# Other orders for the five engines' steps, planned with longer VectorE and GpSimd durations for the first batch

## What is computed

```python
scale, shift = jnp.split(emb @ W_emb + b_emb, 2, axis=-1)
xn = _rms_norm(x, g_norm) * (1.0 + scale) + shift
q, k, v = ...                     # of xn @ W_qkv, 16 heads of 64
q, k = _rms_norm(q, g_q), _rms_norm(k, g_k)
attn = softmax(einsum('bhqd,bhkd->bhqk', q, k) * d ** (-0.5))
o = einsum('bhqk,bhkd->bhqd', attn, v)   # back to (b, n, dim)
return x + o + o @ W_out
```

## Time and profile before

| | us |
|---|---|
| Median of 3 runs | 2257.38 |
| Lowest and highest | 2257.04, 2260.83 |
| Profiled execution, its time: the span from the first to the last instruction, the only one given for it | 2255.9 |
| TensorE busy in the span | 2176.2 |
| VectorE | 1748.6 |
| ScalarE | 1411.7 |
| GpSimd | 931.4 |

### The profile page before, as it was taken

One profiled execution on the slowest core, in us unless ns is written; L12 is line 12 of the kernel. 1 busy time (PEld: TensorE's weight loads), 2 busy tenths in 40 slices (PEclk: granted clock), 3 DMA queues, 4 the chain that ended last, 5 costly groups with the idle time before them and its releaser, 6 DMA issues.

```text
span 2255.9 us, 39472 instructions
## 1 busy us (share of the span) xinstructions
PE 2176.2 (96%) x13392; PEld 1992.2 (88%) x13392; DVE 1748.6 (78%) x3511; ACT 1411.7 (63%) x3077; POOL 931.4 (41%) x1241
## 2 busy tenths in 40 slices
PE   7788789999999999999999999999999999999999
PEld 3676678999999999999999999999999999999989
DVE  4799988678985699767986689857897569876786
ACT  4577766467854577546864578646775458754663
POOL 3866674235532345223541246312553325422330
PEclk9899999999999999999999999999999999999999
DMA  7655464777556765568555675566654775656842
GB/s 299 238 212 226 188 224 147 269 269 254 192 187 241 271 218 196 175 236 289 207 202 197 230 285 192 189 238 242 230 205 165 254 281 199 203 192 227 294 157 103
DMA packets 141528, 497.55 MB, mean 221 GB/s; under 512 B 14864, under 2 KB 61968, under 8 KB 140304
## 3 DMA queue, kind: packets, MB, share of 16 engines
q1 hardware_dynamic: 141328, 495.03, 61.7%
HBM read 425.77 MB, written 69.21 MB: 219 GB/s over the span
## 4 chain that ended last, share of the span: by engine, by line
PE 77%; DVE 11%; issue 4%; DMA 4%; ACT 3%; POOL 1%; SPq 0%; DVEq 0%; ACTq 0%
PE proj_bank L597 16%; PE proj_bank L599 16%; PE proj_bank L598 16%; PE flip_bank L721 8%; PE pv_bank L732 5%; PE pv_bank L733 5%; PE score_bank L713 4%; PE score_bank L714 4%; DMA w_ring<-qkv_store 2%; DVE neg_max L1069 2%; DVE probs L1075 2%; PE score_bank L686 2%; DVE pt_lo L1079 1%; ACT pt_hi L866 1%; ACT probs L860 1%
## 5 line engine op out<-in xcount | busy, mean ns | idle before, releaser
L597 PE MATMUL proj_bank<-w_ring,xa_hi 128*128 128x384 f32 x1792 | 626.5, 350 | 21.0 <-DVE xa_lo L1058 7.6
L599 PE MATMUL proj_bank<-w_ring,xa_lo 128*128 128x384 f32 x1792 | 606.4, 338 | 0.0
L598 PE MATMUL proj_bank<-w_ring,xa_hi 128*128 128x384 f32 x1792 | 605.7, 338 | 0.0
L860 ACT ACTIVATE probs<-score_bank,neg_max 128x512 f32<-128x512 f32 x512 | 352.1, 690 | 250.0 <-DVE neg_max L1069 242.6
L866 ACT CAST pt_hi<-flip_bank 128x512 fp32r<-128x512 f32 x512 | 296.3, 586 | 235.7 <-PE flip_bank L721 148.3
L1079 DVE TENSOR_TENSOR pt_lo<-flip_bank,pt_hi 128x512 fp32r<-128x512 f32 x512 | 346.6, 686 | 117.0 <-ACT pt_hi L866 111.6
L1069 DVE TENSOR_REDUCE neg_max<-score_bank 128x1 f32<-128x512 f32 x512 | 341.4, 684 | 75.0 <-PE score_bank L714 71.7
L597 PEld LDWEIGHTS proj_bank<-w_ring,xa_hi 128*128 128x128 f32 x1792 | 340.6, 190 | 40.8 <-issue 13.5
L598 PEld LDWEIGHTS proj_bank<-w_ring,xa_hi 128*128 128x128 f32 x1792 | 341.3, 190 | 9.6
L599 PEld LDWEIGHTS proj_bank<-w_ring,xa_lo 128*128 128x128 f32 x1792 | 339.6, 190 | 0.0
L721 PE MATMUL flip_bank<-ident,probs 128*128 128x128 f32 x2048 | 294.3, 274 | 14.5 <-DVE probs L1075 7.3
(11 more groups left out here) (91 smaller groups left out, 3855.3 us busy)
## 6 DMA issues: line engine op xcount, KB each, us to landing
w_ring<-qkv_store SPq DMA_DIRECT2D x392, 768.0 KB, 5.7
w_ring<-wo_store SPq DMA_DIRECT2D x108, 512.0 KB, 4.7
qkv_store<-w_ring SPq DMA_DIRECT2D x56, 768.0 KB, 4.9
x_tile<-in_x SPq DMA_DIRECT2D x36, 512.0 KB, 7.8
w_raw<-in_x SPq DMA_DIRECT2D x112, 128.0 KB, 6.4
out<-w_raw SPq DMA_DIRECT2D x112, 128.0 KB, 1.9
w_raw<-in_w_qkv SPq DMA_DIRECT2D x16, 768.0 KB, 7.8
wo_store<-w_ring SPq DMA_DIRECT2D x16, 512.0 KB, 5.0
```

The costliest lines, as they stand in the source:

```text
L597: nc.tensor.matmul(dst, a_hi, w[:, 0, :], start=start, stop=False, skip_group_check=shared)
L598: nc.tensor.matmul(dst, a_hi, w[:, 1, :], start=False, stop=False, skip_group_check=shared)
L599: return nc.tensor.matmul(dst, a_lo, w[:, 0, :], start=False, stop=stop, skip_group_check=shared)
L860: nc.scalar.activation(probs[h][:, i, :], score_bank[n % 2][:, :], ACT.Exp, bias=neg_max[:, n:n + 1], accum_out=row_sum[:, n:n + 1]).then_ ...
```

## The change

All fifteen lists are replaced. Each holds the same steps as before, in another order; no other line of the kernel changes (all lines below the tables move down by 12: line 1178 of before is line 1190 of the changed kernel). The lists are the output of a planner; for this change it was given longer durations for VectorE and GpSimd in the first batch, where both work beside each other on the weights. Two of the lists, cut to the lines that the text speaks of:

```diff
     "GpSimd": """
...
-        X7 0J0 0J1 0J2 0J3 X11 X8 0L4 0L5 0L6 0D0 X12 X10 X9 0J4 0L7 0L8 0J5 0L9 0D1 0L10 0M0 0M1 0L11 0L12 0D2 0D3 0M2
-        0M3 0L13 1D0 1D1 1M0 X13 2L0 2L1 1M1 0V0 2L2 2J0 1D2 1M2 2J1 1D3 2J2 1M3 2L3 2J3 0V1 1V0 2L4 2L5 1V1 2L6 2L7 2J4
...
+        0J0 0J1 X7 0J2 0L4 X11 X8 0L5 0L6 0J3 0J4 0L7 X12 X10 X9 0L8 X13 0L9 0D0 0J5 0L10 0M0 0L11 0D1 0M1 0D2
...
     "SyncE": """
...
-        4H11 4H12 6G3 4H13 6H0 6H1 6H2 6H3 6H4 6H5 6H6 6H7 6H8 6H9 6H10 G0 G1 6H11 6H12 E0 E1 E2 E3 8W0 6H13 8W1 8W2 8W3
...
```

More of the change, by code:

```diff
@@ new lines @@
+    "SyncE": """
+        0H0 0H1 0H2 0H3 0H4 0H5 0H6 0H7 0H8 0H9 0H10 2G0 2G1 2G2 0H11 0H12 2G3 0H13 2H0 2H1 2H2 2H3 +X0 2H4 2H5
+        2H6 2H7 2H8 2H9 2H10 4G0 4G1 4G2 2H11 2H12 4G3 +X1 +X2 2H13 4H0 +X3 4H1 4H2 4H3 4H4 4H5 4H6 4H7 4H8 4H9
+        4H10 6G0 6G1 6G2 4H11 4H12 6G3 4H13 6H0 6H1 6H2 6H3 6H4 6H5 6H6 6H7 6H8 6H9 6H10 G0 G1 6H11 6H12 8W0
+        6H13 8W1 8W2 8W3 8W4 8W5 E0 E1 E2 E3 8W6 8W7 8W8 8W9 8W10 8W11 8W12 8W13 H0 G4 H1 H2 G5 O0 H3 E4 H4 G8
+        H5 O1 O2 H6 E5 G9 H7 E6 O3 10W0 O4 10W1 E7 10W2 10W3 O5 10W4 10W5 10W6 10W7 10W8 10W9 10W10 10W11 10W12
+        O6 10W13 H8 O7 G12 E8 E9 H9 H10 G13 E10 O8 H11 O9 H12 E11 O10 E12 H13 O11 H14 12W0 E13 12W1 O12 H15 O13
+        E14 12W2 E15 12W3 O14""".split(),
@@ L165 @@
-    "SyncE": """
-        -O15 E0 +X0 +X1 +X2 +X3 E1 E2 E3 E4 E5 E6 E7 E8 E9 E10 E11 4W4 4W5 4W6 4W7 4W8 4W9 4W10 4W11 4W12 4W13 6W0 6W1
-        6W2 6W3 6W4 6W5 6W6 6W7 6W8 6W9 6W10 6W11 6W12 6W13 8W0 8W1 8W2 8W3 8W4 8W5 8W6 8W7 8W8 8W9 8W10 8W11 8W12 8W13
-        W0 W1 W2 W3 W4 W5 W6 O0 E12 O1 E13 O2 W7 E14 10W0 10W1 O3 O4 E15 O5 O6 10W2 10W3 O7 10W4 10W5 10W6 10W7 10W8
-        10W9 10W10 10W11 10W12 10W13 W8 W9 W10 W11 W12 W13 W14 O8 O9 O10 W15 12W0 12W1 O11 O12 O13 O14 12W2 12W3""".split(),
+        4C0 4C1 4C2 2W0 4C3 2W1 4C4 2W2 2F4 2F5 2W3 4C5 2F6 2W4 4C6 2W5 2F7 3F0 4C7 2W6 4C8 4C9 2W7 3F1 3S6 3F2
@@ new lines @@
+    "GpSimd": """
+        0Q0 1Q0 +A0 3V0 3V1 4D0 4D1 4M0 +A1 2Q0 +A2 +A3 4M1 4D2 4M2 4D3 4M3 5D0 5D1 5M0 3Q0 5D2 4V0 5M1 4V1 5D3
+        5M2 5M3 +X0 5V0 +X7 5V1 +X1 +X8 6D0 6D1 +X4 6M0 4Q0 +X11 6M1 6D2 6M2 6D3 6M3 7D0 7M0 7D1 6V0 +X5 +X10
+        7D2 6V1 7D3 7M1 7M2 7M3 +X3 +X9 +X12 +X2 7V0 5Q0 7V1 8D0 8M0 8D1 6Q0 +X6 8D2 8M1 8D3 8M2 8M3 +X13 7Q0
+        9D0 9D1 9D2 8V0 9D3 8V1 9M0 9M1 9M2 9M3 9V0 9V1 10D0 10D1 10M0 10D2 10D3 10M1 10M2 10M3 11D0 11D1 11M0
+        11M1 11D2 11M2 11D3 11M3 10V0 10V1""".split(),
@@ new lines @@
+    "SyncE": """
+        +X0 4W4 +X1 4W5 4W6 -O15 4W7 +X2 +X3 4W8 E0 4W9 4W10 4W11 4W12 4W13 6W0 6W1 6W2 E1 6W3 6W4 6W5 E2 E3 6W6
+        6W7 6W8 6W9 E4 6W10 6W11 6W12 6W13 E5 8W0 E6 8W1 8W2 8W3 8W4 8W5 8W6 8W7 8W8 8W9 8W10 8W11 8W12 E7 8W13
+        W0 W1 W2 W3 E8 O0 W4 W5 W6 W7 10W0 O1 10W1 E9 O2 E10 E11 10W2 10W3 10W4 O3 10W5 O4 O5 E12 10W6 10W7 10W8
+        10W9 10W10 E13 O6 10W11 10W12 10W13 O7 W8 W9 W10 W11 W12 W13 O8 W14 W15 O9 O10 E14 12W0 O11 12W1 E15
+        12W2 O12 O13 12W3 O14""".split(),
@@ L199 @@
     "GpSimd": """
[L200 to L201 removed]
+        0Q0 1Q0 3V0 3V1 4D0 2Q0 4D1 4M0 4V0 4D2 4M1 4M2 4D3 4M3 5D0 4V1 5D1 5M0 5M1 5D2 5D3 5M2 5M3 3Q0 5V0 6D0
+        6M0 5V1 6D1 6M1 4Q0 6D2 6D3 6M2 6M3 5Q0 7D0 6V0 7D1 7M0 7M1 7D2 7D3 6V1 7M2 7M3 7V0 7V1 6Q0 7Q0""".split(),
     "SyncE": """
[L203 removed]
@@ L204 @@
-        6W12 6W13 W0 W1 W2 W4 W5 W6 W8 W9 W10 W12 W13 W14 W3 W7 W11 W15 O0 O1 O2 O3 O4 O5 O6 O7 O8 O9 O10 O11 O12 O13
-        O14 O15""".split(),
+        4W4 4W5 4W6 E0 4W7 E1 4W8 4W9 4W10 E2 4W11 -O15 4W12 4W13 6W0 6W1 6W2 6W3 6W4 6W5 6W6 6W7 E3 6W8 6W9
+        6W10 6W11 6W12 6W13 W0 W1 W2 W4 W5 W6 W8 W9 W10 W12 W13 W14 W3 W7 O0 W11 O1 W15 O2 O3 O4 O5 O6 O7 O8 O9
+        O10 O11 O12 O13 O14 O15""".split(),
 }
```

277 lines of the change are left out of this document (137 added, 140 removed).

## The result

The changed kernel takes 2265.68 us (median of 5 runs, 2265.14 to 2268.91), against 2257.38 us of the kernel before (2254.71 to 2260.83). The ratio is 1.0038, with a 95% interval of 1.0025 to 1.0051: it is slower by 8.3 us, where 11 us less were forecast. The result lies outside the range. The profiled execution of the changed kernel is the slowest of its five (2268.91 us), so the differences between the two traces add up to 11.2 us and not to 8.3.

The account below looks back on a forecast made before the run. TensorE was taken as the bound, except VectorE from about 100 to 318 us. Terms -4.7 - 2 - 4.7 + 0 + 0.4 = -11.0 us off the 2255.9 span gave 2244.9, plus 1.5 for the median: 2246.4 us, range 2232 to 2258.

Parts of the forecast that it names:

- term 4: Six middle batches: TensorE's short waits for exponentials and pt_lo taken to change by 0 in sum, bounds -4 and +8 us.
- The criterion at the end of the prediction: Sign of being wrong: early waits gone yet the next batch begins at 490 us, or middle batches over 267 us.
- third rival: Port conflicts decide: more VectorE-GpSimd meetings in the first batch's middle part cancel the gain or slow it; 2261 to 2266 us, 9%.
- Term 1: Start, up to the first score tile: earlier C8 and no wait for X13; -4.7 us, bounds -2 and -7.
- Term 2: First batch, 100 to 318 us: VectorE's own waits of 8.3 us shrink; -2 us, bounds -8 and +8.
- term 3: Second batch's weights, issued ahead of residual loads: TensorE's two waits go; -4.7 us, bounds -2.3 and -4.9.
- Term 5: The end: last weights W11 and W15, issued behind stores O0 and O1, arrive late; +0.4 us, bounds 0 and +3.

Follow-up runs that it names:

- the first run here: The changed kernel's lists for the first batch with the lists of before for the seven others; 2242.97 us, ratio 0.993 to the kernel before.

## Why the prediction was wrong

**The step that failed is term 4**, "0, with bounds -4 and +8", for the six middle batches. Measured: 2094.1 - 476.9 = 1617.2 us against 2082.9 - 489.8 = 1593.1, +24.2 us. I had judged the new middle lists by TensorE's alone, by how close together its own steps that depend on each other stand, and took VectorE's and GpSimd's durations as given. They are not: they depend on which steps of the two meet. I had also said that neither number tells where VectorE stands at that moment, and yet gave a bound of 8 us, a third of what came. What the runs show in its place: VectorE's steps of a middle batch are stretched by 11.0 us in place of 3.6, and TensorE waits for them. The criterion at the end of the prediction (middle batches over 267 us) is the one that was met.

**The third rival had the mechanism and the wrong place.** It counted meetings only between 100 and 318 us, because VectorE is the bound there, and it priced them to 2261 to 2266 us; the median fell there by luck, since the first batch gained 13 us and the middle lost 24. In the first batch the new lists did meet a little more often; in the stretch of the earlier trace rows the groups read

```profile
L1087 DVE TENSOR_SCALAR probs<-probs,row_inv 128x512 f32<-128x512 f32 x50 | 36.1, 722 | 1.8
...
L920 DVE TENSOR_TENSOR w_ring<-w_raw,w_ring 128x384 fp32r<-128x384 f32 x39 | 28.6, 738 | 1.6 <-ACT w_ring L772 1.6
```

against 688 and 719 ns, some 2.5 us in all. The middle batches I had excluded by their idle time, VectorE busy for 205 of 266 us. An idle 60 us of a batch are no cover for 2.8 us that come within six, if they lie on the chain to the next step of TensorE. The rule of the Trainium skill (SBUF — State Buffer, Who interferes with whom) that the prediction set beside this rival, whole instructions in turn, fits the rows from 829 to 838 us above: each of the three stretched steps ends 0.3 to 0.5 us behind a step of GpSimd. It does not fit GpSimd's 128x4 steps, beside which a scaling keeps its 487 ns (the last section); there the measurement decides.

**Term 1, the start: -4.7 forecast, -1.1 in the changed kernel**, short even of the bound of -2 (counted from TensorE's first step of the batch: -1.3 there, -2.2 to -2.7 in six of the seven others with this first batch, +0.6 in the seventh). Its first half assumed that C8 starts 2 us earlier, since less of VectorE's work stands ahead of Y2, at the durations of the earlier trace rows. But G3 to G7 now ran beside GpSimd's weight steps and its operands, and C8 started 0.7 us later than before. VectorE (x2 is two steps in a row), then C8:

```profile
58.03 2.91 DVE L1019 TENSOR_TENSOR x_tile<-x_tile 128x512 f32<-128x512 f32 x2
...
64.95 3.41 DVE L1019 TENSOR_TENSOR x_tile<-x_tile 128x512 f32<-128x512 f32 x2
...
69.06 0.66 PE L609 MATMUL proj_bank<-w_ring,xa_hi 128*128 128x384 f32 x1 [8.25 <-issue]
```

1.45 and 1.7 us for a G that I had taken at 0.68. And even where C8 came 7 us earlier nothing followed, as the run with Y2 early shows. The second half assumed 7.1 us from the turn to the low part of k; in the run with X13 early it was 9.3 us (87.9 to 97.2), and why is open. The wait for X13 did go, as forecast, but the chain behind the turn was nearly as late.

**Term 2, the middle of the first batch: -2 forecast; measured** -5.4 + 1.1 = -4.3 us up to the first score of pair 5, within the bounds. I put VectorE's time up to 6S0 into three heaps by adding its steps at their undisturbed durations, the stretch and the idle time: before 237 + 36 + 30 us, after 237 + 39 + 22 (without the last wait, for the score itself, which belongs to term 3). The order bought 8 us less idle time for 3 us more stretch. The forecast took 2 us off the waits. VectorE's waits in the stretch of the earlier trace rows are now

```profile
DVE neg_max L1081 <- PE score_bank L726: 2.1, 2, 1.2
...
DVE pt_lo L1091 <- ACT pt_hi L878: 0.8, 4, 0.3
```

2.9 us in place of 8.3: of these two kinds 5.4 us went.

**Term 3, the weights of the second batch: -4.7 forecast, -3.6 measured alone**, within its bounds. In the changed kernel the loads from 8W1 on are issued from 301.73, right behind the store 6H13, and the first score of pair 6 comes at 312.05 behind the low part of k:

```profile
301.73 7.13 SPq L1278 DMA_DIRECT2D w_ring<-qkv_store  x4
...
312.05 0.47 PE L725 MATMUL score_bank<-k_hi,q_split 128*128 128x512 f32 x1 [0.44 <-DVE k_lo L1051]
```

**Term 5, the end: +0.4 forecast, 0.0 measured** (173.1 us for the last batch in both).

The first batch by terms 1 to 3 was forecast at -11.4 us and gave -13.0 in the changed kernel, some -16 in most others. That sum is near by luck, because errors in it cancel: the start was put 3.6 us too large and the middle 2.3 too small. From the first score of pair 5 on, the changed kernel gained another 7.6 us, where term 3 had 4.7: 5.6 of them up to the first score of pair 6, and 2.0 behind it, where the prediction had nothing.

## What to carry to other kernels

Where two engines hold each other up, an order has to be judged on both lists at once: lay the SBUF-to-SBUF steps of VectorE beside the wide steps of GpSimd at the times of the trace, and count the pairs, in every stage and not only in the one where VectorE is the bound. Idle time in the mean is no cover: three stretched steps, one close behind the other, cost TensorE 2 us in a batch in which VectorE is idle for 59. A change that consists of several tables is worth splitting by table before anything else: the first run here found a version that is 0.7% faster than the kernel before inside one that is 0.4% slower.

## What the runs showed of the hardware

How exact the meetings are. The five batches from the second to the sixth of the changed kernel hold 320 scalings of 128x512 on VectorE.

- 160 overlap nothing on GpSimd and take 487 ns (485 to 490).
- 60 overlap only 128x4 or smaller steps of GpSimd and take 487 ns as well: these do not hold VectorE up, not even the inverse root, 1.03 us in the mean.
- 80 start while a wide step of GpSimd (128x256 or 128x512) runs, and are held up: 988 ns in the mean, up to 1555. Every one of them ends 279 to 289 ns behind the end of a wide step. 15 sums G were held up too, and end 545 to 552 ns behind one.
- 20 touch a wide step and still take 487 ns. In 15 of them the wide step starts 0.1 to 0.4 us behind the scaling; the other 5 start 0.15 us before one ends.

In the kernel before, 30 of 320 scalings were held up, for 811 ns in the mean. So there are 10 more per middle batch, and longer ones: 6.1 us of the 7.4 us of added stretch, and the sums G make up nearly all of the rest. Row maxima, low parts of turned tiles and evictions, each with at least one operand in PSUM, take the same time beside a wide step as alone (685 ns in both cases for the low parts).
